# Who issues the second strips of a count matrix: moving SBUF-to-SBUF transfers from ScalarE's queue to GpSimd's, with the pieces of the aggregation spread anew

## The reference

```
n  = layernorm(x)
h  = relu(n @ W1 + b1) @ W2 + b2              # 512 -> 256 -> 512
x  = x + h + segment_sum(h[dst], src)         # row = src, col = dst
t  = layernorm(x)
g  = softmax(t @ Wg + bg) - 0.25 * sigmoid(t @ Wt + bt)
w  = max(g, 0) / sum(max(g, 0))               # 8 experts, all of them computed
x  = x + sum_e w[:, e] * (t @ We[e] + be[e])  # We[e] is 512 x 512
```

## Time and profile before

| | |
|---|---|
| median of 3 runs | 368.37 us (366.07 to 368.53) |
| the profiled execution | 368.55 us, span of the core 366.7 us |
| mean granted TensorE clock | 0.985 |
| busy | PE 93%, DVE 81%, ACT 33%, POOL 15% |
| span outside the engines' instructions | 1.85 us (368.55 less 366.7) |

### The profile page before, as it was taken

One profiled execution on the slowest core, in us unless ns is written; L12 is line 12 of the kernel. 1 busy time (PEld: TensorE's weight loads), 2 busy tenths in 40 slices (PEclk: granted clock), 3 DMA queues, 4 the chain that ended last, 5 costly groups with the idle time before them and its releaser, 6 DMA issues.

```text
span 366.7 us, 7571 instructions
## 1 busy us (share of the span) xinstructions
PE 342.5 (93%) x2618; PEld 260.7 (71%) x2618; DVE 296.9 (81%) x571; ACT 120.3 (33%) x231; POOL 54.7 (15%) x102
## 2 busy tenths in 40 slices
PE   1799999799897999999999999999999999999995
PEld 1688885565443445466767888888888888888884
DVE  7599998768956687897797888888888888888764
ACT  6798653542424212477631303003030030200000
POOL 5000000000000000063823223050130500500000
PEclk9999999969989999999999999999999999999999
DMA  7964122223322250003000012030030300000133
GB/s 163 244 176 150 42 64 57 54 55 81 78 61 59 73 149 17 0 1 122 2 1 0 2 24 93 2 117 0 5 113 1 116 1 2 2 1 2 47 113 123
DMA packets 23813, 22.08 MB, mean 60 GB/s; under 512 B 15978, under 2 KB 16775, under 8 KB 23776
## 3 DMA queue, kind: packets, MB, share of 16 engines
q1 hardware_dynamic: 18212, 18.72, 18.2%
q10 hardware_dynamic: 5564, 2.87, 3.2%
HBM read 12.77 MB, written 2.56 MB: 42 GB/s over the span
## 4 chain that ended last, share of the span: by engine, by line
PE 80%; DVE 5%; ACT 4%; issue 4%; ACTq 2%; DMA 1%; SPq 1%; DVEq 0%
PE ps_g L1336 10%; PE ps_g L1337 10%; PE ps_g L1338 10%; PE ps_g L1155 9%; PE ps_w L1203 6%; PE ps_g L1140 4%; PE ps_a L1336 2%; PE ps_a L1338 2%; PE ps_a L1337 2%; PE ps_w L1336 2%; PE ps_w L1337 2%; PE ps_w L1338 2%; ACTq L386 2%; PE ps_g L1260 2%; DVE x_sb L940 2%
## 5 line engine op out<-in xcount | busy, mean ns | idle before, releaser
L1030 DVE SCALAR_TENSOR_TENSOR x_sb<-ps_g,weight_s,x_sb 125x256 f32<-125x256 f32 (+1 forms) x142 | 75.2, 547 | 19.5 <-PE ps_g L1338 18.4
L834 DVE TENSOR_TENSOR split<-places,keys 125x756 f16<-125x756 int16 (+4 forms) x119 | 74.5, 678 | 19.4 <-PE ps_w L1203 17.4
L1336 PE MATMUL ps_g<-wb_hi,places 128*128 128x256 f16 x212 | 57.8, 273 | 0.1
L1338 PE MATMUL ps_g<-wb_hi,r_sb 128*128 128x256 f16 x212 | 57.8, 273 | 0.0
L1337 PE MATMUL ps_g<-wb_lo,places 128*128 128x256 f16 x212 | 57.8, 273 | 0.0
L1155 PE MATMUL ps_g<-late,r_sb 125*128 125x512 f32 (+3 forms) x120 | 54.1, 563 | 0.8 <-DMA late<-counts 0.8
L1203 PEld LDWEIGHTS ps_w<-split 125*128 125x128 f16 x476 | 30.2, 99 | 16.1 <-issue 8.6
L1203 PE MATMUL ps_w<-split 125*128 125x125 f16 x476 | 36.3, 221 | 4.5 <-DVE split L834 2.7
L1336 PE MATMUL ps_g<-wb_hi,split 128*128 128x256 f16 x142 | 38.7, 273 | 0.0
L1337 PE MATMUL ps_g<-wb_lo,split 128*128 128x256 f16 x142 | 38.7, 273 | 0.0
L1338 PE MATMUL ps_g<-wb_hi,split 128*128 128x256 f16 x142 | 38.7, 273 | 0.0
(11 more groups left out here) (229 smaller groups left out, 675.9 us busy)
## 6 DMA issues: line engine op xcount, KB each, us to landing
stage<-in_L_ffn_W_exp_dram SPq DMA_DIRECT2D x8, 1024.0 KB, 5.2
late<-counts SPq DMA_DIRECT2D x60, 58.6 KB
x_sb<-in_x_dram SPq DMA_DIRECT2D x5, 448.0 KB, 12.2
out_dram<-x_sb SPq DMA_DIRECT2D x10, 224.0 KB
late<-counts ACTq DMA_DIRECT2D x35, 58.6 KB
w_sb<-in_L_gnn_W_dram SPq DMA_DIRECT2D x2, 512.0 KB, 11.0
out_dram<-x_sb ACTq DMA_DIRECT2D x10, 26.0 KB
b_sb<-in_L_gnn_b_dram SPq DMA_DIRECT2D x1, 250.0 KB
```

The source lines that it names most:

```text
L834: nc.vector.tensor_tensor(hot[hot_at(stage, p)][:, 0:n, :].rearrange("p c (k x j) -> p c k x j", k=SEGS, j=2), places_of(windows[s], n), k ...
L1030: nc.vector.scalar_tensor_tensor(out=x_sb[:, i, a:z], in0=bank[0:R, at:at + z - a], scalar=weight_s[:, expert_of(u), i:i + 1], in1=x_sb[:, ...
L1336: nc.tensor.matmul(out_cols, hi_x, wb_hi[par][:, q, k, :], start=(opens and k == 0), stop=False, skip_group_check=True)
L1338: mm = nc.tensor.matmul(out_cols, lo_x, wb_hi[par][:, q, k, :], start=False, stop=(k == 1), skip_group_check=True)
```

## The change

Five edits. GpSimd's queue gets a loop that issues strip 1 of every group from 8 on (before: SyncE for groups 8 to 13, ScalarE from 14), with a set of semaphores of its own that `moved` and `block_out` wait for as well. The pieces of tile 0 go two to a group behind groups 13 to 15, those of tile 1 behind 16 to 20. ScalarE's last nine table pieces come behind every second group from 14 on, its weight conversions a group later, and the last of them in two halves behind groups 42 and 44. On TensorE the row ends are multiplied out behind the first set of keys and ahead of the second, and the first turned tile of x comes after both; ScalarE takes the moments of tile 0 between the two sets of keys; VectorE sets its registers before it waits.

```diff
@@ names and planning
-        ACT_MOVES = 14
+        POOL_MOVES = 8
+        LATE_PIECES = 14
@@ def move
+            landed = pool_moved[q] if by_pool(g, strip) else win_moved[q]     # by_pool: s == 1 and g >= POOL_MOVES
...
-                                  counts[q][...]).then_inc(win_moved[q], 16)
+                                  counts[q][...]).then_inc(landed, 16)
@@ def moved
                 eng.wait_ge(win_moved[q], MOVED_BY[tile][q])
+                if MOVED_POOL_BY[tile][q]:
+                    eng.wait_ge(pool_moved[q], MOVED_POOL_BY[tile][q])
@@ block.sync
-                if g < ACT_MOVES:
+                if g < POOL_MOVES:
                     move(sp, g, 1, begun)
@@ block.gpsimd
+            begun = [2]
+            for g in range(POOL_MOVES, NG):
+                pool.wait_ge(win_out, g + 1)
+                move(pool, g, 1, begun)
@@ block.scalar, block_out
                     act.wait_ge(win_moved[q], MOVED[g - RINGS])
+                    if MOVED_POOL[g - RINGS]:
+                        act.wait_ge(pool_moved[q], MOVED_POOL[g - RINGS])
@@ block.scalar, between the two sets of keys
+            moments(0)
             act.wait_ge(keys_turned, 2)
...
-            for i in range(MOMENTS_AHEAD):
+            for i in range(1, MOMENTS_AHEAD):
@@ block.scalar, high_blocks: expert 1's sums in two halves (n = 2 and 3)
+                if n >= 2 and e == 1:
+                    a = T1 + 2 * (n - 2)
+                    act.wait_ge(t_added, 4)
+                    nc.scalar.activation(hi[:, a:a + 2, :, :], t_sum[:, a - T1:a - T1 + 2, :, :], ...)
@@ block.scalar, the loop over groups
                 block_out(g)
-                if g >= ACT_MOVES:
-                    act.wait_ge(win_out, g + 1)
-                    move(act, g, 1, begun)
-                if 1 + PIECES_AHEAD + MOMENTS_AHEAD + g - first_out < PIECES:
-                    table(1 + PIECES_AHEAD + MOMENTS_AHEAD + g - first_out)
-                if g in (38, 40, 42):
+                if g >= LATE_PIECES and g % 2 == 0 and pieces_done < PIECES:
+                    table(pieces_done)
+                    pieces_done += 1
+                if g in (38, 40, 42, 44):
                     high_blocks(1, (g - 38) // 2)
-                if g == 33:
+                if g == 34:
                     (line 659)
-                if g == 35:
+                if g == 36:
                     (line 662)
@@ block.vector: five reg_mov from behind wtab to ahead of wait_ge(wrows_ready, 1)
@@ block.tensor, the start
-            for a, (key, bank) in enumerate(((lo_f, ps_w[0]), (pos_f, ps_w[1]))):
-                (turn the keys)
+            turn_keys(0, lo_f, ps_w[0])
+            pe.wait_ge(ends_ready, 1)
+            (the two products of line 1121, then_inc(wrows_ready, 1))
+            turn_keys(1, pos_f, ps_w[1])
...
+            pe.sem_inc(hot_used, 1)
             turn_x(0)
-            pe.wait_ge(ends_ready, 1)
-            (the two products of line 1121, then_inc(wrows_ready, 1))
-            pe.sem_inc(hot_used, 1)
             turn_x(1)
@@ block.tensor, pieces
                     if i == 0:
-                        g = SLOTTED + n // 3
+                        g = SLOTTED + n // 2
                     if i == 1:
-                        g = SLOTTED + 2 + n // 2
+                        g = max(g, SLOTTED + 3)
```

More of the change, by code:

```diff
@@ L268, in gnn_moe @@
         win_moved = [sem(f"win_moved{q}") for q in range(RINGS)]
+        pool_moved = [sem(f"pool_moved{q}") for q in range(RINGS)]
         a_summed = sem("a_summed")
@@ L360, in gnn_moe @@
         MOVES, MOVED, MOVED_BY, LAST = [], [], {}, {}
-        total = [0] * RINGS
+        total, total_pool = [0] * RINGS, [0] * RINGS
+        MOVED_POOL, MOVED_POOL_BY = [], {}
         for g in range(NG):
@@ L370, in gnn_moe @@
             MOVES.append(moves)
-            total[g % RINGS] += 16 * len(moves)
+            later = sum(s == 1 and g >= POOL_MOVES for s, a, z, tile, at in moves)
+            total[g % RINGS] += 16 * (len(moves) - later)
+            total_pool[g % RINGS] += 16 * later
             MOVED.append(total[g % RINGS])
+            MOVED_POOL.append(total_pool[g % RINGS])
             for s, a, z, tile, at in moves:
@@ L375, in gnn_moe, with by_pool @@
                 MOVED_BY[tile] = list(total)
+                MOVED_POOL_BY[tile] = list(total_pool)
+        def by_pool(g, s):
+            return s == 1 and g >= POOL_MOVES
         def move(eng, g, strip, begun):
             q = g % RINGS
+            landed = pool_moved[q] if by_pool(g, strip) else win_moved[q]
             for s, a, z, tile, at in MOVES[g]:
@@ L386, in move @@
                     eng.dma_start(a_t[tile % 3][at:at + z - a, :].rearrange("p (h l) -> p h l", h=HI),
-                                  counts[q][SHIFT + a * HI:SHIFT + z * HI, s * LO:(s + 1) * LO]).then_inc(win_moved[q], 16)
+                                  counts[q][SHIFT + a * HI:SHIFT + z * HI, s * LO:(s + 1) * LO]).then_inc(landed, 16)
         def moved(eng, tile):
@@ L763, in _ @@
                                     AX_X, ALU.max).then_inc(ends_ready, 1)
+            word_reg = dve.alloc_register("dve_word")
+            turn_reg = dve.alloc_register("dve_turn")
+            end_reg = [dve.alloc_register(f"dve_end{s}") for s in range(4)]
+            need_reg = dve.alloc_register("dve_need")
+            dve.reg_mov(turn_reg, 0)
+            for s in range(4):
+                dve.reg_mov(end_reg[s], 0)
             dve.wait_ge(wrows_ready, 1)
@@ L784, in _ @@
             nc.vector.tensor_tensor(wtab[:, 0:NG], row_span[:, :], row_from[:, :], ALU.add).then_inc(wtab_ready, 1)
[L786 to L792, removed]
             dve.wait_ge(wtab_ready, 2)
@@ L918, in low_block @@
                 of = {B11: w[:, 0:2, 0:H], B21: w[:, 2:4, 0:H], B22: w[:, 2:4, H:D]}
-                dve.wait_ge(wb_hi_done, 3 * (e - 1) + (1 if q == B11 else 2 if q <= B22 else 3))
+                dve.wait_ge(wb_hi_done, 3 * (e - 1) + (1 if q == B11 else 2 if q <= B22 else 3) + (1 if e > 1 or q >= T1 + 2 else 0))
                 nc.vector.scalar_tensor_tensor(out=wb_lo[e % 2][:, q, :, :], in0=of[q] if q <= B22 else t_sum[:, q - T1, :, :],
@@ L1099, in _, with turn_keys @@
             turned.then_inc(hits_turned, 1)
-            for a, (key, bank) in enumerate(((lo_f, ps_w[0]), (pos_f, ps_w[1]))):
+            def turn_keys(a, key, bank):
                 pe.wait_ge(keys_ready, a + 1)
@@ L1105, in _ @@
                 turned.then_inc(keys_turned, 1)
+            turn_keys(0, lo_f, ps_w[0])
+            pe.wait_ge(ends_ready, 1)
+            for a in range(2):
+                row = nc.tensor.matmul(ps_a[0:1, a * NV:(a + 1) * NV], wmax[:, a:a + 1], ident[0:NV, 0:NV], start=True, stop=True)
+            row.then_inc(wrows_ready, 1)
+            turn_keys(1, pos_f, ps_w[1])
             def turn_x(i):
@@ L1116, in turn_x @@
                 t.then_inc(x_turned, 1)
+            pe.sem_inc(hot_used, 1)
             turn_x(0)
-            pe.wait_ge(ends_ready, 1)
-            for a in range(2):
-                row = nc.tensor.matmul(ps_a[0:1, a * NV:(a + 1) * NV], wmax[:, a:a + 1], ident[0:NV, 0:NV], start=True, stop=True)
-            row.then_inc(wrows_ready, 1)
-            pe.sem_inc(hot_used, 1)
             turn_x(1)
```

6 lines of the change are left out of this document (4 added, 2 removed).

## The result

The changed kernel takes 353.7 us (median of 4 runs, 353.34 to 354.47), beside 367.31 for the kernel before (now the median of 4, a fourth having come at 366.26): ratio 0.963, 95% interval 0.959 to 0.968. The prediction was 356.4. The profiled execution took 354.47 us with a span of 352.6, so 14.1 us less than that of before.

A forecast was written before the change was run, and what follows sets the result against it. The prediction took ScalarE's cycle of copy, DMA issue and table piece to pace the counting of groups 13 to 53. From 368.5 us it took 11.1 for the stage and 1.0 for the start: 356.4 us, range 352 to 371.

The forecast's parts named there:

- The size of the stage's gain: Counting of groups 13 to 53, copy to copy: 63.1 us instead of 74.2, so 11.1 us gained.
- Its base: Same stage: the slower of TensorE and VectorE in each part, 58.6 us, before waits that no engine's work explains.
- third extra: Stage: short pieces (226, 286 columns) leave TensorE's sequencer about 0.1 us behind, 16 times, 1.5 us.
- the conversion (1): Stage: the conversion of line 659 stays whole, 1.91 us on ScalarE, so TensorE waits about 1 us.
- VectorE's waits for landings (2): Stage: VectorE waits for landed strips before column sums, 2.3 us in the profile, 2 kept in the sum.
- GpSimd's queue: Groups 13 to 52: 44 issues at an assumed 1.27 us, 56 us, hidden just under the stage's 63.
- the break-even: GpSimd's issue cost above which the kernel gets slower: 74.2 us over 44 issues, 1.69 us each.
- The start: Before counting: row ends and table earlier, third turned tile some 1.0 us sooner; gain 1.0 us, between 0 and 1.6.
- The tail: After the stage: GpSimd's last strip lands no later unless GpSimd is behind; the following 230 us shift as they are.
- Rival 1: GpSimd paces the stage mildly at 1.5 to 1.6 us an issue: stage 68 us, time 361.4; chance 0.10.
- rival 2: VectorE operations hold up GpSimd's issues, 1.92 us each: stage 84.5 us, time 378; chance 0.17.
- Rival 3: Stage engines and landing strips wait for each other, clock falls: 5 us of clock or 4 of waits, 361; chance 0.10.

The follow-up runs named there:

- rest_no_pool: Changed kernel with strip 1 issued as before, by SyncE up to group 13 and by ScalarE from 14: 363.99 us, stage 70.2 us.
- pool_only: Kernel before with only the queue changed, GpSimd issuing strip 1 from group 8 on: 358.07 us, stage 62.9 us.
- old_tables: Changed kernel with table pieces behind each of groups 13 to 21 and conversions as before, the last as two halves behind group 42: 355.14 us.
- sum_lag8: Changed kernel with VectorE's column sums one group later (SUM_LAG 8 for 7): 353.42 us, stage 60.4 us.
- pool_x2: Changed kernel with each of GpSimd's strips cut into two DMAs: 360.90 us, stage 60.1 us.
- pool_x3: Changed kernel with each of GpSimd's strips cut into three DMAs of a third of the rows: 375.16 us, stage 73.1 us.
- run 20: Not a follow-up run: the words say that TensorE ran 20 one-column matmuls after waiting for a strip; no time of its own.

## Why the prediction was right

*What bounded the stage.* Right, shown by rest_no_pool and pool_only: ScalarE's cycle of copy, DMA issue and table piece. It had to be read from the queue's rows, since ScalarE was 37% busy by the windows.

*The size of the stage's gain*, 11.1 predicted, 14.0 measured, so the stage took 60.2 us where the prediction's sum had 63.1 and its signs "61 to 65". Its base, the slower of TensorE's and VectorE's work in each part, was 58.6, and that it lies so near is partly luck. The changed stage cut at copy 29:

```profile
56.28:81.69 25.41, 25.37 (x194) 15.67 (x193) 23.86 (x35) 12.10 (x25) 10.37 (x18) 1.00 0.30 71
81.69:116.51 34.82, 33.78 (x226) 19.73 (x224) 28.35 (x48) 14.46 (x31) 14.78 (x26) 1.00 0.40 86
```

In groups 14 to 29 the prediction had VectorE as the slower, with 26.7 us; they took 25.4, and TensorE was the full engine. Groups 30 to 53 took 34.8 where it had TensorE's 31.9. TensorE's own work was priced too low, 55.1 us for the stage, and it was busy 59.2. Two things are missing from the price. A group with two pieces takes 2.38 us (copies at 98.58 and 100.96) against 0.49 + 964 x 1.68 ns = 2.11; it has a second diagonal product (line 1215). And behind a 226-column piece the next count comes late:

```profile
102.14 0.49 PE L1230 MATMUL ps_w<-split 125*128 125x125 f16 x6
102.47 0.60 PE L1182 MATMUL ps_g<-late,r_sb 125*128 125x226 f32 x2
102.91 0.27 PE L1211 MATMUL ps_w<-self_lo,self_pos 128*128 128x250 f16 x1
103.45 0.50 PE L1230 MATMUL ps_w<-split 125*128 125x125 f16 x6 [0.26 <-issue]
```

The two counts are 1.31 us apart, where the price has 0.49 + 226 x 1.68 ns = 0.87: about 0.4 us, and so at each of the last four such pieces. That is the prediction's third extra (the sequencer, 1.5 us in all): it was there, with 1.6 us in these four alone. Of the other two extras, the conversion (1) cost nothing, because it fell beside two pieces of TensorE; in its old place it cost just that 1 us (old_tables). VectorE's waits for landings (2) grew to 5.2 us, of which sum_lag8 took away 1.7 without an effect; TensorE had no idle time in the first part and 1.0 us in the second, so they had hardly a place in the sum. From the sum to the measured time it is 356.4 - 2.9 (stage) - 0.7 (start) + 1.5 (behind the stage) = 354.3: the errors partly offset one another.

*The clock.* Taken as full, and it was 1.00. What I left open was which part lifts it: in the profiled executions either did, the queue or the order of pieces.

*Pieces and tables.* The gap of the pieces was balance between VectorE and TensorE, 0.9 us. "Nothing" for the table pieces was right: old_tables runs level with the changed kernel until group 33. "Nothing" for the two halves was right where they stand; back to back they cost 0.6 us. What the prediction did not see is that the long conversion, moved by one group, costs nothing either.

*GpSimd's queue.* I took 1.27 us an issue, from bounds of 0.78 and 2.33; it is 0.57, below the lower end. It did not matter, because the argument was the break-even: the issues were hidden at 0.6 us a strip and at 1.2 (pool_x2), and paced the stage at 1.75 (pool_x3). The Trainium skill's page "DMA: Bandwidth & Descriptors" has about 1 us to the first byte on this path (section "Latency and other measured facts"); the trace has no first byte, but the whole way from issue to landing, 2.7 us.

*The start.* 1.0 predicted, 1.7 measured. ScalarE's moments of tile 1 began at 14.34 us, where those of tile 0 had begun at 14.22 before: almost a whole tile's moments (1.8) had been fitted ahead, into the idle 1.25 us that I counted and the gaps around the keys that I did not.

*The tail.* "Shifts as it is" missed 1.5 us of the profiled execution, a lower clock in the last tile's matmuls. It is not in every execution: from copy 53 to the end sum_lag8 took 351.6 - 116.6 = 235.0 us, 0.4 more than the kernel before. My sentence on the last strip was right for this kernel, but it missed the expert's load: pool_x2 shows that 2 us later it would have cost five.

*The rivals.* Rival 1 (1.5 us an issue) and rival 2 (hold-up by VectorE) did not happen. Rival 2's mechanism exists for copies: the copies took the longest issue from 737 to 1045 ns, the additions left it at 737. The page "SBUF — State Buffer" of the Trainium skill (section "Who interferes with whom") says that copies can take the port pair that GpSimd shares and that `tensor_tensor` has no two-port mode. The traces show no ports, but the delays agree with both. By its summary's advice (section "Summary: rules for kernel authors"), to issue such DMAs from ScalarE or SyncE instead, this kernel would be at 363.99 or 369.62 us and not at 353.70. Rival 3 wanted 4 to 5 us on top of my sum; the stage came 2.9 below it.

## What to carry to other kernels

An engine whose queue issues DMAs can pace a loop at 37% busy: add the issue times to its cycle before believing a releaser. Ask of a second queue how much of its time one turn of the loop takes against the loop's period, and what else sits in front of its last transfer, above all a large load that another queue issues as soon as it is free. Small works on an engine off the bound cost nothing here while they fitted into the bound's turns (table pieces, 0.0 us), and a long one cost 1 us in one place and nothing one group later, so long ones belong beside the bound's longest turn. And a computed stage time that comes out near the measured one is worth cutting in two: here each half was off, in opposite directions.

## What the runs showed of the hardware

- A DMA issue of 120 runs of 500 bytes took 0.57 us on GpSimd, 0.77 on SyncE and 0.78 on ScalarE. On GpSimd 40 runs took the same.
- A strip took 2.7 us from GpSimd's issue to landing (2.3 to 3.7). The last half strip took 5.8 us when a 1 MB load had been issued 0.1 us before it, and 2.2 with that load held back.
- VectorE's float32 copies of 621 ns lengthened GpSimd's issues to up to 1045 ns, one of them to 0.12 us behind the copy's end; additions of 627 ns did not (737 at most, as without them).
- The granted clock went low (0.84 in 11 us) behind the stage in the profiled execution of the changed kernel, with TensorE busy 10.5 of those 11 us, and did not in the kernel before or in sum_lag8. In all three TensorE had waited for a strip just ahead of it (0.83, 0.60 and 0.83 us) and then run 20 one-column matmuls, so these alone don't decide it. What does was not tried.
